# Overlapping the local attention of two batches in a fused two-layer kernel

## The chip, the cores and the metric

The kernel runs on one core of a Trainium2 chip. The metric is the device time of one execution in microseconds; lower is better. Times are told as the median of several runs, and one more execution was taken by the hardware profiler.

## What is computed

The input is x, 8 batches of 512 tokens with 128 channels. Each of two layers is `x = x + s(xn) * silu(f(xn))` with `xn = layernorm(x)`. Only layer 0 has local attention, and the change is mostly there:

```python
# layer 0, s: windowed attention in 64 channels, two branches of 32 channels
xi = rmsnorm(x @ down_w + down_b, norm1_w)
o1 = branch(xi[..., :32], window=10, shift=5)     # 8 heads of 4, relative bias, mask at the wrap
o2 = branch(xi[..., 32:], window=20, shift=10)
x  = x + concat(o1, o2) @ up_w + up_b
s  = x + gelu(rmsnorm(x) @ ffn_w1 + ffn_b1) @ ffn_w2 + ffn_b2
# layer 0, f: 8 experts, the best 2 for each token, and a shared expert (swiglu, width 128)
f  = sum_e cw[t, e] * expert_e(xn[t]) + shared(xn[t])
# layer 1: s is full attention of 16 heads, f is a mixture of 8 experts (width 352), the best 2
```

In a branch, each window of w tokens has a w x w score table for each head: scores plus bias, -100 where the shift has wrapped tokens of both ends into the last window, then softmax, times v, and a projection.

## The kernel before

Tokens lie on partitions, 128 at a time, so a batch is 4 tiles (NT) and all is 32 tiles (TILES). For the windowed attention a batch is folded into 4 groups of windows, so that (group, channel) fill the 128 partitions and the score tables lie along the free dimension in one tile `WS` of 1300 (window 10) + 2800 (window 20) elements.

`plan0()` writes out the order of layer 0 by hand as one list. It begins with statistics, normalisation and the down projection of all batches, then `("route",)`, the routing of all tokens, then a row of slots, which are simply concatenated. Each engine walks the same list and does its own part of each item, in order, with semaphores between engines. So an item that waits holds back everything behind it on that engine.

The items of the slots:

- `("window", b, n)`, n = 0..18 (`FRONT` = 19 slots, one batch after another). n = 0 to 2: the rmsnorm of `XIR` (VectorE squares and sums, GpSimd takes the power, VectorE scales into `XI`). n = 3, 4: TensorE transposes, ScalarE evacuates to `XIT`, TensorE makes q, k, v, ScalarE evacuates to `QKV`. n = 5 to 11: ten chunks; for a chunk, VectorE multiplies q and k into `G` (line 1350), TensorE sums over a head's channels with `HEADSUM` into bank 4 or 5 of PSUM (line 623), VectorE adds the bias into `WS` (line 1341). In a chunk's life these are at slots n, n+1 and n+2. n = 10, 11: VectorE adds `MASK` to the last window on 32 partitions (line 1307) and takes the maximum of each row (1308); GpSimd subtracts it for window 20 (1099), VectorE for window 10. n = 12, 13: ScalarE exponentials. n = 13, 14: VectorE sums and reciprocals (1312, 1314), and for window 10 also the product with v and the output. n = 15: GpSimd multiplies with v for window 20 (1105). n = 18: VectorE's last reduction (1320).
- `("tail", b, k)`, k = 0..6 (`TAIL_AT`): projection, up projection and residual, rmsnorm (ScalarE squares, GpSimd power, VectorE scale), transposes, the two halves of ffn1 with gelu, ffn2. `up_b` and `ffn_b2` are added by a matmul with one row (`ONES` x `ROWS`, lines 572 and 656).
- expert passes k = 0..30: 8 for the shared expert, 23 over blocks of 512 sorted rows. A pass is `sorted` (transposes), `pair` (8 matmuls, line 673), `gate` (two evacuations by ScalarE, two by VectorE at 1393, two clamps at 1397 and 1400, a silu by ScalarE), `act` (1407), `down_e` (TensorE, line 691) and `yev` (VectorE, 1420). Passes begin every 4, 5, 5, 5 slots.
- `("send", g)`: GpSimd issues two indirect DMAs (line 1124), one tile of tokens to its place among the sorted rows. `("split", b)` prepares the weights of layer 1: ScalarE rounds, VectorE subtracts (1425), SyncE stores.

The heart of the plan:

```python
for n in range(FRONT):
    slots[FRONT * b + n].append(("window", b, n))
...
slots[at].append(("pair", k)); slots[at + 1].append(("gate", k)); slots[at + 3].append(("act", k))
slots[at + 5].append(("down_e", k)); slots[at + 6].append(("yev", k))
at += (4, 5, 5, 5)[k % 4]
```

One batch's scores, its `QKV` tile and banks 4 and 5 are single, so the next batch's q, k, v come only after this batch's output. Layer 1 has a plan of the same kind; its routing is one item at slot `ROUTE_AT` = 50, and GpSimd waits there for the positions.

Of the kernel before, what the change touches and what calls it, by code (L numbers as in the profile page):

```python
# [28 lines left out]
FRONT = 19  # L29
# [21 lines left out]
TAIL_AT = {1: 0, 3: 1, 5: 2, 7: 3, 9: 4, 11: 5, 13: 6}  # L51
# [5 lines left out]
def plan0():  # L57
# [9 lines left out]
    out.append(("route",))  # L67
    count = FRONT * B + 40
# [24 lines left out]
def plan1():  # L93
# [23 lines left out]
    put(ROUTE_AT, ("route",))  # L117
    for g in range(TILES):
        put(ROUTE_AT + 2 + g, ("send", g))
# [68 lines left out]
def turns0(plan):  # L188

    uses = []  # L190
    for what, *a in plan:
        if what == "norm":
            uses.append(("xnt", a[0]))
        elif what == "route":
# [3 lines left out]
        elif what == "tail" and a[1] != 2:  # L198
            uses.append((("proj", "up", None, "h", "ffn1a", "ffn1b", "ffn2")[a[1]], a[0]))
# [3 lines left out]
def turns1(plan):  # L203

    uses = []
    for what, *a in plan:
        if what == "norm":
            uses.append(("xnt", a[0]))
        elif what == "route":
# [30 lines left out]
def build(nc, A):  # L240
    ctx = ExitStack()
    with ctx:
# [21 lines left out]
        NHALF = sb("NHALF", [128, NT])  # L264
# [8 lines left out]
        VAR = sb("VAR", [128, NT])  # L273
# [12 lines left out]
        with ExitStack() as one:  # L286
# [12 lines left out]
            UPW = sb0("UPW", [64, 128])  # L299
            ROWS = sb0("ROWS", [1, 3, 128])  # L300
# [3 lines left out]
            MASK = [sb0(f"MASK{r}", [128, WIN[r], WIN[r]]) for r in range(2)]  # L304
# [8 lines left out]
            ZERO = sb0("ZERO", [128, 1024])  # L313
# [5 lines left out]
            TH = sb0("TH", [128, 2, T])  # L319
            YE = sb0("YE", [128, 2, NT, 128])  # L320
            XIR = sb0("XIR", [128, TILES, 64])
            SQT = sb0("SQT", [128, NT, 64])
            SQ = sb0("SQ", [128, 2, NT])
            RSTD = sb0("RSTD", [128, 3, NT])
            XI = sb0("XI", [128, NT, 64])
            XIT = sb0("XIT", [64, XIT_W])
            QKV = [sb0(f"QKV{r}", [128, 3, GRP[r]]) for r in range(2)]
            G = sb0("G", [128, 2, 512])
            WS = sb0("WS", [128, S_W])
            WM = [sb0(f"WM{r}", [128, GRP[r]]) for r in range(2)]  # L330
            WO = [sb0(f"WO{r}", [128, GRP[r]]) for r in range(2)]
            PPT = sb0("PPT", [64, T])
# [74 lines left out]
        def _(sp):  # L407
# [25 lines left out]
            load(ROWS[:], A["rows"], "w_b")  # L433
# [748 lines left out]
        def _(dve):  # L1182
# [140 lines left out]
            def window(b, n):  # L1323
# [27 lines left out]
                if n == 10:  # L1351
                    window_max(1)
# [310 lines left out]
```

## Time and profile before

| | |
|---|---|
| median of 3 runs | 1742.53 us (1740.51 to 1747.9) |
| the profiled execution | 1744.1 us, of which 1742.3 us are the span of the profile |
| VectorE busy | 1111.4 us (64%) |
| TensorE busy | 1167.2 us (67%), mean granted clock 0.765 |
| ScalarE busy | 684.7 us (39%) |
| GpSimd busy | 453.8 us (26%) |
| down projections of all batches end | 63 us |
| routing ends, first window item | 90 us |
| period of one batch in layer 0 | 78.5 us, the same for six batches |
| end of layer 0 | 738.5 us |

A busy share is a mean over stages; in layer 0 the six equal periods between 206 and 678 us are the part to look at. TensorE's busy time depends on its granted clock, 0.5 or 1.0 of 2.4 GHz at any moment; a mean lies between.

### The profile page before, as it was taken

How to read it: one execution, taken by the hardware profiler on the slowest of the kernel's cores; microseconds unless marked ns; L12 is line 12 of the kernel's file. 1: busy time of each engine (PE TensorE's matmuls, PEld its weight loads, DVE VectorE, ACT ScalarE, POOL GpSimd, SP SyncE). 2: the span in 40 equal slices, each digit the busy share in tenths (PEclk: the TensorE clock that was granted, in tenths of full speed). 3: DMA queues.
4: the chain of work that ended last, by engine and by line, in shares of the span. 5: the costliest groups of instructions: out<-in, count | busy, mean ns of one | idle time of the engine just before them, and what ended most of it. 6: DMA issues, size and time to landing. Idle time of an engine off the chain costs nothing.

```text
span 1742.3 us, 17058 instructions
## 1 busy us (share of the span) xinstructions
PE 1167.2 (67%) x5494; PEld 630.5 (36%) x5494; DVE 1111.4 (64%) x1856; ACT 684.7 (39%) x1166; POOL 453.8 (26%) x412
## 2 busy tenths in 40 slices
PE   4464665757585765532456647699997778787886
PEld 4332333434343432311122222288882323232331
DVE  3566758585857657215577586466667878677761
ACT  1112333333323333120223436443445766656663
POOL 2156611120202111243444147500003303213110
PEclk9967868777777868555556769599998888788885
DMA  8210212121221110016033124556544333253400
GB/s 281 101 59 27 71 52 67 43 83 33 83 67 58 62 40 29 6 26 81 17 56 50 18 44 98 113 169 200 200 150 74 49 45 55 41 77 45 73 20 7
DMA packets 73726, 125.03 MB, mean 72 GB/s; under 512 B 13541, under 2 KB 31014, under 8 KB 73638
## 3 DMA queue, kind: packets, MB, share of 16 engines
q1 hardware_dynamic: 65446, 107.15, 25.5%
q0 software_dynamic: 8192, 16.79, 4.0%
q8 instruction: 44, 0.72, 0.2%
q14 instruction: 44, 0.36, 0.1%
HBM read 57.74 MB, written 40.37 MB: 56 GB/s over the span
## 4 chain that ended last, share of the span: by engine, by line
PE 42%; DVE 23%; issue 12%; POOL 10%; ACT 8%; DMA 3%; SPq 2%; DVEq 0%; ACTq 0%; POOLq 0%
PE PS L770 5%; PE PS L813 5%; PE PS L673 5%; PE PS L623 4%; POOL XS1D L1163 4%; PE PS L790 4%; PE PS L832 4%; PE PS L573 3%; ACT P L880 3%; PE PS L750 2%; DVE MX L1553 2%; DVE WS L1307 2%; POOL YG L1147 2%; PE PS L578 2%; PE PS L736 2%
## 5 line engine op out<-in xcount | busy, mean ns | idle before, releaser
L1553 DVE TENSOR_REDUCE MX<-PS 128x1 f32<-128x512 f32 x512 | 323.8, 685 | 132.5 <-PE PS L750 123.5
L880 ACT ACTIVATE P<-PS 128x512 f32<-128x512 f32 x512 | 278.0, 596 | 194.8 <-PE PS L790 192.7
L790 PE MATMUL PS<-QS,KS 50*128 50x512 f32 x512 | 138.2, 536 | 103.6 <-ACT P L880 98.1
L750 PE MATMUL PS<-KS,QS 48*128 48x512 f32 x512 | 149.3, 580 | 66.9 <-DVE MX L1553 40.5
L770 PE MATMUL PS<-P,V 128*32 128x512 f32 x1024 | 180.3, 786 | 0.0
L1147 POOL DMA_INDIRECT A<-Y1D,POS x64 | 73.5, 1148 | 281.2 <-DMA Y1D<-YE 190.8
L750 PEld LDWEIGHTS PS<-KS,QS 48*128 48x128 f32 x512 | 58.0, 224 | 218.7 <-DVE MX L1553 112.6
L790 PEld LDWEIGHTS PS<-QS,KS 50*128 50x128 f32 x512 | 60.0, 230 | 165.5 <-ACT P L880 138.8
L623 PE MATMUL PS<-G,HEADSUM 128*128 128x400 f32 (+2 forms) x160 | 81.2, 639 | 51.5 <-DVE WS L1341 50.6
L673 PE MATMUL PS<-XST,WB 128*128 128x512 f32 x184 | 106.2, 732 | 4.4 <-issue 4.4
L813 PE MATMUL PS<-XRH,WH 128*128 128x512 f32 (+1 forms) x276 | 103.1, 414 | 0.2 <-DVE A L1495 0.2
L1169 POOL TENSOR_TENSOR MAG<-MAG,EH 128x1024 f32<-128x1024 f32 x8 | 19.0, 2369 | 265.2 <-ACT MAG L880 216.7
L1105 POOL TENSOR_TENSOR WS<-WS,QKV 128x2800 f32<-128x2800 f32 x8 | 48.8, 6102 | 131.8 <-DVE WM L1312 131.8
L1099 POOL TENSOR_TENSOR WS<-WS,WM 128x2800 f32<-128x2800 f32 x8 | 39.5, 4940 | 165.1 <-DVE WM L1308 165.1
L1350 DVE TENSOR_TENSOR G<-QKV 128x400 f32<-128x400 f32 (+1 forms) x80 | 46.1, 586 | 54.4 <-PE PS L623 48.9
L1124 POOL DMA_INDIRECT XS0D<-XN,POS x64 | 64.7, 1011 | 54.5 <-issue 52.8
L832 PEld LDWEIGHTS PS<-W,A 128*128 128x128 f32 (+1 forms) x552 | 71.9, 191 | 6.5
L832 PE MATMUL PS<-W,A 128*128 128x128 f32 (+1 forms) x552 | 72.4, 274 | 0.0
L880 ACT ACTIVATE TH<-PS 128x512 f32<-128x512 f32 (+1 forms) x69 | 41.2, 598 | 76.3 <-PE PS L813 76.2
L880 ACT ACTIVATE H<-PS,WB 128x512 f32<-128x512 f32 x46 | 30.9, 687 | 101.5 <-PE PS L673 101.5
L1491 DVE SCALAR_TENSOR_TENSOR SL<-TH,PS 128x512 f32<-128x512 f32 (+1 forms) x69 | 47.1, 683 | 36.1 <-ACT TH L880 36.1
L691 PE MATMUL PS<-WB,AA 128*128 128x128 f32 x184 | 35.5, 354 | 51.7 <-DVE AA L1407 51.7
(208 smaller groups left out, 2222.3 us busy)
## 6 DMA issues: line engine op xcount, KB each, us to landing
WH<-W1SD SPq DMA_DIRECT2D x23, 704.0 KB, 4.3
QS<-EH SPq DMA_DIRECT2D x64, 128.0 KB
KS<-EH SPq DMA_DIRECT2D x64, 128.0 KB
WB<-in_wb SPq DMA_DIRECT2D x23, 322.0 KB, 2.8
XS<-XS0D SPq DMA_DIRECT2D x23, 256.0 KB, 2.7
Y0D<-YE SPq DMA_DIRECT2D x23, 256.0 KB, 2.0
XS<-XS1D SPq DMA_DIRECT2D x23, 256.0 KB, 3.7
Y1D<-YE SPq DMA_DIRECT2D x23, 256.0 KB, 2.7
```

Of the source, the lines that this page charges most:

```text
L623: signal(pe.matmul(PS[:, 4 + c % 2, 0:width], HEADSUM[:], G[:, c % 2, 0:width], start=True, stop=True), "S")
L673: ins = pe.matmul(PS[:, 2 * pair + m, :], w[:, at:at + 128], x, start=True, stop=True)
L750: signal(pe.matmul(PS[:, s % 4, :], QS[rows, u % 3, hp, 128 * t:128 * t + 128], KS[rows, u % 3, hp, :], start=True, stop=True), "ms")
L770: ins = pe.matmul(PS[32 * a:32 * a + 32, 6, :], V[:, u // 2 % 2, k, at:at + 32], P[:, m % 2, a, :], start=k == 0, stop=k == NT - 1)
L790: signal(pe.matmul(PS[:, 4 + s % 2, :], KS[rows, u % 3, hp, 128 * k:128 * k + 128], QS[rows, u % 3, hp, :], start=True, stop=True), "st")
L813: ins = pe.matmul(out, WH[:, j % 2, w, f:f + m], x[:, j % 2, :], start=n == 0, stop=n == 2)
L832: ins = pe.matmul(PS[:, 4 + j % 2, 128 * t:128 * t + 128], A4[0:m, q % 3, 128 * t:128 * t + 128], W2[0:m, j % 2, c, :], start=c == 0 and t ...
L880: act.activation(*a, **k).then_inc(sem[name], 1)
L1124: pool.indirect_dma_start(XS0D, bass.IndirectOffsetOnAxis(POS[0][:, k, g:g + 1], 0), XN[:, g, :], None).then_inc(sem["sent"], 16)
L1147: pool.indirect_dma_start(dst[:, k, t, :], None, src, bass.IndirectOffsetOnAxis(pos[:, k, g:g + 1], 0)).then_inc(sem[name], 16)
L1163: pool.indirect_dma_start(XS1D, bass.IndirectOffsetOnAxis(POS[1][:, k, g:g + 1], 0), XN[:, g, :], None).then_inc(sem["sent1"], 16)
L1553: go("mx", dve.tensor_reduce(MX[:, u % 2, t, 4 * par + hp:4 * par + hp + 1], PS[:, s % 4, :], AX.X, ALU.max))
```

## The change

- The plan of layer 0 has a period: the window items of batch b begin at slot `PERIOD * b` with `PERIOD` = 9 and still take 19 slots, so items of two or three batches share a slot, the older batch first. `WS` and `QKV` have two buffers. The tail of a batch has 8 steps at slots 19 to 27 of it.
- Passes begin every 3 slots, and their items follow each other in neighbouring slots. With `PERIOD` = 9 that is 3 passes in a period.
- The rmsnorm after the down projection is done once for all 32 tiles, in a new item `("xi",)` ahead of the slots, in place in `XIR`. GpSimd then builds the bias tables, too.
- The mask is added to the bias of the last window ahead of time (`LAST`), so that the addition in the chunk's evacuation takes it along; the two additions at line 1307 go.
- The one-row matmuls go: `up_b` is a 65th row of `UPW` against a row of ones in `PPT`; `ffn_b2` is added to `X1` by GpSimd (tail step 3).
- The subtraction of `split` moves from VectorE to GpSimd.
- The routing is in 7 parts in slots 0 to 6 (in layer 1: 50 to 56); the sends begin at slot 8, two tiles in a slot (in layer 1: at 58 rather than 52, one in a slot), and GpSimd waits for the positions only there. The trigonometric tables of layer 1 move from ahead of the slots to slot 27.
- `window_sum` and what follows it come one slot later. `TH` is gone, the silu writes in place.

```diff
-FRONT = 19
+FRONT, PERIOD = 19, 9
-TAIL_AT = {1: 0, 3: 1, 5: 2, 7: 3, 9: 4, 11: 5, 13: 6}
+TAIL_AT = {0: 0, 1: 1, 2: 2, 4: 3, 5: 4, 6: 5, 7: 6, 8: 7}
+ROUTE_PARTS = 7
...
-    out.append(("route",))
+    out.append(("xi",))
...
-            slots[FRONT * b + n].append(("window", b, n))
+            slots[PERIOD * b + n].append(("window", b, n))
         for n, k in TAIL_AT.items():
-            slots[FRONT * (b + 1) + n].append(("tail", b, k))
-        slots[FRONT * b + 9].append(("split", b))
+            slots[PERIOD * b + FRONT + n].append(("tail", b, k))
+        slots[PERIOD * b + 9].append(("split", b))
+    for n in range(ROUTE_PARTS):
+        slots[n].append(("route", n))
     for g in range(TILES):
-        slots[g].append(("send", g))
+        slots[ROUTE_PARTS + 1 + g // 2].append(("send", g))
+    slots[ROUTE_PARTS + 20].append(("trig",))
...
-        slots[at + 3].append(("act", k))
-        slots[at + 5].append(("down_e", k))
-        slots[at + 6].append(("yev", k))
-        at += (4, 5, 5, 5)[k % 4]
+        slots[at + 2].append(("act", k))
+        slots[at + 3].append(("down_e", k))
+        slots[at + 4].append(("yev", k))
+        at += (3,3,3)[k % 3]
```

```diff
 # TensorE, tail: the one-row matmuls
-                    signal(tok_matmul(ntok(out), PPT, UPW[:], ROWS[:, 0]), "aux_full")
+                    signal(tok_matmul(ntok(out), PPT, UPW[:]), "aux_full")
...
-                        pe.matmul(out[:, t], ONES[0:1, :], ROWS[:, 1], start=True, stop=False)
 # VectorE, window: the mask
-                step(dve.tensor_tensor(s, s, MASK[r][96:128].rearrange("p q k -> p (q k)"), ALU.add))
...
+                        if w <= (PADT // WIN[r] - 1) % NWIN[r] < w + m:
+                            bias = LAST[r][:].rearrange("p w q k -> p w (q k)")
+                        else:
+                            bias = bc(BIAS[r][:].rearrange("p q k -> p (q k)"), [128, m, a], 1)
 # ScalarE, window n = 4: q, k, v of the next batch no longer wait for this one's output
-                    if b:
-                        act.wait_ge(sem["wout0"], b)
-                        act.wait_ge(sem["wout1"], b)
+                    if b >= 2:
+                        act.wait_ge(sem["wout0"], b - 1)
+                        act.wait_ge(sem["wout1"], b - 1)
 # GpSimd
+                elif what == "xi":
+                    pool.wait_ge(sem["xi_sq"], 1)
+                    rsqrt(RSTDX[:], SQX[:], 1.0 / 64, 1e-6, "rstd_xi")
...
+                        go("init_p", pool.tensor_tensor(last, last, bc(BIAS[r][:].rearrange("p q k -> p (q k)"),
+                                                                       [128, (3, 1)[r], w * w], 1), ALU.add))
...
+                elif what == "tail" and a[1] == 3:
+                    pool.wait_ge(sem["h0"], a[0] + 1)
+                    go("x1_b", pool.tensor_tensor(X1[:], X1[:], bc(FB2[:], [128, NT, 128], 1), ALU.add))
+                elif what == "split":
+                    pool.wait_ge(sem["split_hi"], a[0] + 1)
+                    go("split_lo", pool.tensor_tensor(SPL[:], STAGE[:], SPH[:].bitcast(F32), ALU.subtract))
 # VectorE, once for all tiles
+                    step(dve.tensor_tensor(sq, XIR[:], XIR[:], ALU.mult))
+                    go("xi_sq", dve.tensor_reduce(SQX[:], sq, AX.X, ALU.add))
+                    dve.wait_ge(sem["rstd_xi"], 1)
+                    go("xi", dve.tensor_tensor(XIR[:], XIR[:], bc(RSTDX[:], [128, TILES, 64], 2), ALU.mult))
+                    dve.wait_ge(sem["init_p"], 5)
```

## Rows read from the trace of the kernel before

**Rows 1.** Windows: busy us of each engine, instructions, granted TensorE clock, DMA share, GB/s.

```profile
285.07:363.60 78.53, 52.30 (x222) 30.67 (x221) 53.07 (x65) 25.93 (x43) 13.46 (x7) 0.76 0.20 62
...
718.30:747.00 28.70, 12.80 (x32) 7.42 (x32) 2.08 (x3) 4.62 (x12) 7.68 (x9) 0.50 0.05 13
...
1003.00:1022.50 19.50, 5.27 (x20) 2.17 (x20) 14.52 (x48) 3.61 (x8) 0.01 (x1) 0.59 0.00 0
```

**Rows 2.** Groups of VectorE from 90 to 745 us: busy us, mean ns, idle before.

```profile
L1393 DVE SCALAR_TENSOR_TENSOR UL<-PS,WB,H 128x512 f32<-128x512 f32 x46 | 33.4, 747 | 30.2 <-ACT H L880 30.2
L1307 DVE TENSOR_TENSOR WS<-WS,MASK 32x100 f32<-32x100 f32 x8 | 32.5, 4066 | 0.3
...
L1407 DVE SCALAR_TENSOR_TENSOR AA<-UL,TH 128x512 f32<-128x512 f32 x31 | 21.3, 686 | 2.5 <-DVE X L1372 2.1 <-ACT TH L880 0.4
...
L1400 DVE TENSOR_SCALAR UL<-UL 128x512 f32<-128x512 f32 x31 | 13.0, 418 | 0.0
...
L1314 DVE RECIPROCAL WM<-WM 128x140 f32<-128x140 f32 x8 | 8.2, 1028 | 0.3
...
L1425 DVE TENSOR_TENSOR SPL<-STAGE,SPH 128x704 fp32r<-128x704 f32 x8 | 7.1, 884 | 0.0
...
L1307 DVE TENSOR_TENSOR WS<-WS,MASK 32x400 f32<-32x400 f32 x8 | 4.6, 571 | 0.3
```

**Rows 3.** Timeline, VectorE and GpSimd in one period: start us, length us.

```profile
285.07 4.08 DVE L1307 TENSOR_TENSOR WS<-WS,MASK 32x100 f32<-32x100 f32 x1
...
312.63 1.23 DVE L1397 TENSOR_SCALAR UL<-UL 128x512 f32<-128x512 f32 x1
...
284.10 4.94 POOL L1099 TENSOR_TENSOR WS<-WS,WM 128x2800 f32<-128x2800 f32 x1 [25.06 <-DVE WM L1308]
307.47 6.11 POOL L1105 TENSOR_TENSOR WS<-WS,QKV 128x2800 f32<-128x2800 f32 x1 [18.43 <-DVE WM L1312]
```

**Rows 4.** Timeline of TensorE in one period.

```profile
644.40 2.92 PE L610 MATMUL PS<-XIT,WQKV 64*32 64x130 f32 x48 [0.93 <-ACT XIT L880]
...
649.10 5.90 PE L673 MATMUL PS<-XST,WB 128*128 128x512 f32 x8 [0.73 <-issue]
...
663.60 3.01 PE L623 MATMUL PS<-G,HEADSUM 128*128 128x400 f32 x4 [1.84 <-DVE WS L1341]
...
674.55 3.60 PE L673 MATMUL PS<-XST,WB 128*128 128x512 f32 x8
...
696.94 2.08 PE L691 MATMUL PS<-WB,AA 128*128 128x128 f32 x8 [12.86 <-DVE AA L1407]
```

**Rows 5.** Groups of ScalarE from 90 to 745 us.

```profile
L880 ACT ACT_TABLE_LOAD x30 | 38.5, 1283 | 0.5
...
L880 ACT ACTIVATE WS<-WS 128x1300 f32<-128x1300 f32 x8 | 10.3, 1286 | 0.1
```

**Rows 6.** Groups of GpSimd from 90 to 745 us.

```profile
L1124 POOL DMA_INDIRECT XS0D<-XN,POS x64 | 64.7, 1011 | 54.5 <-issue 52.8 <-POOL RSTD L1078 0.6 <-POOL WS L1099 0.6
...
L1078 POOL TENSOR_TENSOR RSTD<-VAR,NHALF 128x4 f32<-128x4 f32 x8 | 8.2, 1020 | 0.7
```

**Rows 7.** A group of TensorE from 90 to 745 us (that of line 572 is alike).

```profile
L656 PE MATMUL PS<-ROWS,ONES 1*128 1x128 f32 x64 | 16.7, 343 | 6.2 <-ACT GL L880 6.2
```

**Rows 8.** Timeline: bias copies, last down projection, first and last step of routing, layer's end.

```profile
49.33 4.28 POOL L1117 COPY BIAS<-RPB 128x10 f32<-128x10 f32 x30
...
62.91 0.42 DVE L1459 TENSOR_TENSOR XIR<-PS,DOWNB 128x256 f32<-128x256 f32 x1 [2.99 <-PE PS L573]
...
68.46 0.42 DVE L1224 TENSOR_REDUCE RS<-PS 128x32 f32<-128x256 f32 x1
...
89.57 0.42 DVE L1284 TENSOR_REDUCE GW<-RT 128x32 f32<-128x256 f32 x1
...
737.85 0.69 DVE L1382 TENSOR_TENSOR XN<-PS,X 128x512 f32<-128x512 f32 x1 [15.32 <-PE PS L658]
```

**Rows 9.** Timeline of VectorE in layer 1, after the sends.

```profile
1116.62 1.23 DVE L1543 CAST EH<-MAG 128x2048 fp32r<-128x2048 f32 x1 [10.01 <-POOL MAG L1170]
```

More of the change, by code:

```diff
@@ L197, in turns0 @@
             uses.append(("xs", a[0]))
-        elif what == "tail" and a[1] != 2:
-            uses.append((("proj", "up", None, "h", "ffn1a", "ffn1b", "ffn2")[a[1]], a[0]))
+        elif what == "tail" and a[1] not in (2, 3):
+            uses.append((("proj", "up", None, None, "h", "ffn1a", "ffn1b", "ffn2")[a[1]], a[0]))
     return {use: n for n, use in enumerate(uses)}
@@ L303, in build @@
             BIAS = [sb0(f"BIAS{r}", [128, WIN[r], WIN[r]]) for r in range(2)]
-            MASK = [sb0(f"MASK{r}", [128, WIN[r], WIN[r]]) for r in range(2)]
+            LAST = [sb0(f"LAST{r}", [128, (3, 1)[r], WIN[r], WIN[r]]) for r in range(2)]
             FW1 = sb0("FW1", [128, 256])
@@ L567, in aux, with tok_matmul @@
                 return PS[:, 7, :]
-            def tok_matmul(out, lhs, rhs, row=None):
+            def tok_matmul(out, lhs, rhs):
                 for t in range(NT):
-                    if row is not None:
-                        pe.matmul(out[:, t], ONES[0:1, :], row, start=True, stop=False)
-                    ins = pe.matmul(out[:, t], lhs[:, 128 * t:128 * t + 128], rhs, start=row is None, stop=True)
+                    ins = pe.matmul(out[:, t], lhs[:, 128 * t:128 * t + 128], rhs, start=True, stop=True)
                 return ins
@@ new lines, in route @@
+                if part == 4:
+                    ps, free = bank_filled(dve, "prefix") if L else (aux_filled(dve, "prefix"), sem["aux_free"])
+                    freed = (SHARED if L else AUX)["prefix",] + 1
+                    counts = lambda n: ps[:, TILES * E * n:TILES * E * (n + 1)].rearrange("p (t e) -> p t e", e=E)
+                    dve.wait_ge(sem["hot" + pre], 1)
+                    dve.tensor_copy(RT[:, 6], counts(0))
+                    step(dve.tensor_copy(RT[:, 7], counts(1)))
+                    dve.tensor_copy(RT[:, 5], counts(1)).then_inc(free, 1)
+                    dve.wait_ge(free, freed)
+                    at, to = 7, 8
+                    for s in (1, 2, 4, 8, 16):
+                        dve.tensor_copy(RT[:, to, 0:s], RT[:, at, 0:s])
+                        step(dve.tensor_tensor(RT[:, to, s:], RT[:, at, s:], RT[:, at, 0:TILES - s], ALU.add))
+                        at, to = to, at
@@ new lines, in route @@
+                if part == 6:
+                    for k in range(2):
+                        step(dve.tensor_tensor(RT[:, 8], RT[:, 3 + k], RT[:, 7], ALU.mult))
+                        step(dve.tensor_reduce(RS[:, k], RT[:, 8], AX.X, ALU.add))
+                        go("pos" + pre, dve.tensor_copy(POS[L][:, k], RS[:, k]))
+                        dve.wait_ge(sem["pos" + pre], k + 1)
+                    for k in range(2):
+                        step(dve.scalar_tensor_tensor(RT[:, 8], RT[:, 3 + k], scale, RT[:, 1], ALU.mult, ALU.mult))
+                        go("gw" + pre, dve.tensor_reduce(GW[L][:, k], RT[:, 8], AX.X, ALU.add))
+                        dve.wait_ge(sem["gw" + pre], k + 1)
@@ L1344, in window @@
                         r, w, m = CHUNKS[c]
-                        q, kk = (QKV[r][:, j, :].rearrange("p (w q) -> p w q", q=WIN[r])[:, w:w + m] for j in range(2))
+                        q, kk = (QKV[r][:, b % 2, j, :].rearrange("p (w q) -> p w q", q=WIN[r])[:, w:w + m] for j in range(2))
                         full = [128, m, WIN[r], WIN[r]]
@@ L1476, in _ @@
                     expert_out(*a)
-                elif what == "split":
-                    split(*a)
             layer0_over(dve)
```

315 lines of the change are left out of this document (147 added, 168 removed).

## The prediction

> **What bounds the kernel now.** I read the windows by stage first, then the groups of each engine in layer 0, then the timeline of one period engine by engine, and last the chain that ended last. Layer 0's slots run from 90 to 738.5 us [rows 8]. Six batches there take 78.5 us each, the same to a hundredth; one of them is [rows 1], first row. In it VectorE is busy for 53.1 of 78.5 us and TensorE for 52.3, at a granted clock of 0.76. So no engine is full. The reader should see in the same row that ScalarE (25.9) and GpSimd (13.5) are far from full too: what bounds the period is the alternation of in-order queues, with 25.4 us in which VectorE waits. After the last window there is a stretch that nothing covers: from 718 to 738 us VectorE is busy for 2.1 us and TensorE runs at 0.50 (second row) [rows 1]. And from 63 to 90 us VectorE does tables and routing alone [rows 8].
>
> **A lock that is easily missed.** The mask addition on 32x100 elements takes 4.07 us, that on 32x400 elements 0.57 us [rows 2]. The small one starts at 285.07 us while GpSimd's subtraction (284.10 to 289.04) is running, and ends with it, at 289.15 [rows 3]. A clamp beside GpSimd's product takes 1.23 us in place of 0.42 and ends when that ends [rows 2, 3]. So a GpSimd tile operation holds back VectorE operations that read two SBUF tiles, and clamps, until it is over. The evacuations (PSUM and SBUF) ran beside it unharmed. The Trainium skill says the same in "SBUF — State Buffer", section "SBUF: two separate sides": the pair of ports that VectorE and GpSimd share is an exclusive lock held for a whole instruction. The trace agrees (4.07 against 0.57 us). By that rule the two operations that this change gives to GpSimd are not free for VectorE wherever a product stands beside them; the sum below counts the lock from the rows.
>
> **The change, VectorE's work.** From 53.07 us in a period go: the mask additions, 4.07 + 0.57 [rows 2]; the split's subtraction, 0.88 [rows 2]; the rmsnorm of XI, three operations on 128x256 at 0.42, 1.26 [rows 8]; the blocked part of a clamp, 1.23 - 0.42 = 0.81 [rows 3]; and one pass in four, since a period now has 3 passes: 2 x 0.747 + 2 x 0.418 + 2 x 0.686 (yev is as long as act) = 3.70 [rows 2]. That leaves 41.8 us.
>
> **Its waits.** I walk through the 9 slots of a period (numbered 1 to 9) in the order of the queues (older batch, younger batch, pass), starting at the end of the gate in the third slot.
> (a) Slots 4 to 6: VectorE has act, h0 and the sum, product and output of window 10, but these need the exponential. ScalarE has the silu, four squares, a table load of 1.28 and the exponential of 1.29 first [rows 5]. Wait at least 1.3; with the squares I take 3.0. The chain XIT, 2.92 us of q, k, v matmuls [rows 4], QKV ends at about the same time as this VectorE work, so it is hidden.
> (b) The gate in slot 6 waits for its pair, which stands behind those 48 matmuls and a down_e on TensorE. TensorE has idled before, so I take the pair of 5.90, not of 3.60 [rows 4], and down_e at 2.08: wait 4.3.
> (c) Slot 7: the sum over window 20 releases GpSimd's product of 6.1 us [rows 3]. Behind the sum VectorE has the reciprocal (1.03 [rows 2]) and then the q, k products of the younger batch, which read two SBUF tiles. They stand for 6.1 - 1.0 = 5.1 us.
> (d) Slot 9: products 6 and 7 need the sums of chunks 4 and 5, which stand on TensorE behind chunks 2 and 3 (up to 3.0 for two [rows 4], here 2.1), down_e 1.7, a pair of some 5.5, half of ffn1 and their own matmul, some 1.6: 12 us after the lock opens. VectorE has 5.3 us of its own meanwhile: wait 6.6.
> (e) Slot 3: the up projection stands behind down_e and a pair (4.7, between the two of [rows 4]), 8.4 us in all against 4.4 us of VectorE's: wait 4.0.
> Period: 41.8 + 3.0 + 4.3 + 5.1 + 6.6 + 4.0 = 64.8, taken as 65. What TensorE is spared is mostly in its shadow: the one-row matmuls are 16.7 + 16.7 us in all [rows 7], 4.2 a batch, of which only the four in front of the up projection are in (e). GpSimd's new operations: at 4.94 us for 2800 elements [rows 3], 704 take 1.2 and 512 take 0.9. They fall beside evacuations and reductions as I lay it out, so I cost them at nothing; if that cover is gone they cost their length. For GpSimd itself, 13.5 us a period grows by 2 in 65.
>
> **Start.** XIR is complete at 63.3 [rows 8]. Two small operations 0.4, squares and sum over 2048 elements, each between the 1.23 of a cast of that size [rows 9] and 8 x 0.42 [rows 8], taken as 2.2; GpSimd's power: 1.02 us for 4 columns [rows 6], for 32 columns between that and 8 x 1.02; I take 2, near the floor. Then GpSimd copies the bias, 4.28 [rows 8], which used to be hidden, and adds two LAST tables (700 elements, 1.3 by the rate above). VectorE scales XIR in that time. All queues wait for this: 63.3 + 0.4 + 4.4 + 2.5 + 4.3 + 2.0 = 77, taken as 78 (bounds 76 and 84). So slots start at 78, not at 90, but the routing, 68.5 to 90.0 [rows 8], is now inside them.
>
> **Slots.** There are 96 of them, the last pass being number 30 at 3 x 30 + 1, with its yev four later. Period 0 (routing 19 us, three passes 11, half a window 7, waits 5): 42. Period 1 (no tails): 57. Periods 2 to 7: 65 each, plus 4 in the third, and 3 in the fourth for the tables. The 4 are for the sends: 64 at 1.01 us and 0.3 us between [rows 6], 81 us, plus 22 us of window work in the same queue, 103 us for slots 8 to 23 of the plan (numbered from 0), against about 107 us that the others need there; the first sorted pass stands in slot 24 right behind and still has its rows to load. Period 8 has no young batch: 44. Period 9 has the last tail and three passes: 37. Two more passes: 20. The last store: 3. Sum: 42 + 57 + 6 x 65 + 7 + 44 + 37 + 20 + 3 = 600, so layer 0 ends at 678 rather than 738.5: 60.5 us less. Each us of the period is worth about 7 us.
>
> **Layer 1.** The routing was a block of 19.5 us in which TensorE was busy for 5.3 (third row) [rows 1]; and behind the sends VectorE waited 10.0 us for a GpSimd product that stood behind all of them [rows 9]. In parts, the one is filled by attention, and the product gets in before the last sends. Against it, positions come later and the sends begin 6 slots later, and at 81 us their length sets when the first rows can be loaded. Bounds 0 and 20 less; I take 7, near the floor, since the sends bind.
>
> **Sum.** 1744.1 - 60.5 - 7 = 1676.6 for an execution like the profiled one; the median of the runs is 1.6 lower: 1675 us.
>
> **Rivals.**
> 1. TensorE stays fast. It has fewer gaps, its clock rises from 0.76 to near 1, and pairs take 3.6 us: 2.3, 1.9 and 1.1 less in (b), (d), (e), and 0.7 from the chunk sums, 6 in all. Period 59, time 1633. For it: pairs of 3.60 exist. Against: its work falls from 52.3 to about 41 us in 65, so its share (63%) is no higher than now (67%). 24%.
> 2. The waits (a), (b), (d), (e) fall under other work, and VectorE is the bound but for the lock: 41.8 + 5.1 + 2 = 49. Time 1675 - 16 x 7 = 1563. Against: its queue is in order, and each wait above is of one queue on another that can't be overtaken. 7%.
> 3. The lock bites everywhere: GpSimd's subtraction (4.9), split (1.2) and bias (0.9) each meet a product or a clamp. 7 more, period 72, time 1725. For it: in the period now both big GpSimd operations do meet one [rows 3]. 14%.
> 4. The other side: TensorE becomes the bound at half clock. Three pairs at 6, five times 3.0 for the chunks, three down_e at 2.1, 2.9 for q, k, v and some 16 for tail and transposes are 58 us; with the stretches in which it must wait for VectorE's reductions (some 18) the period is 76 and the time 1752. It decides from a period of 75. For it: 0.50 in the lone tail [rows 1]. Against: at the same share of work the clock is 0.76 now. 5%.
> 5. The change doesn't overlap: a bank or a tile that is still single (banks 4 and 5, the shared bank 7, WM, WO) makes the batches follow each other, and the saved operations are paid back by the bunched passes. Time 1742. 3%.
>
> **How the numbers follow.** The forecast as laid out, 1655 to 1700, has 47%, and 1675 is its middle. The range of 8 in 10 reaches over most of rival 1 and a part of rival 3: 1620 to 1715. It takes in the bounds of start and layer 1 (+6, +7 and -13) and 5 us of the period either way. A measurement of this kernel can tell about 0.5%, 9 us, from no change. Faster by more: 47 + 24 + 7 + 14 = 92%; within: 3%; slower: 5%.
>
> **What would show it.** Slots start (first routing step) near 78 us. Six periods of about 65 us. VectorE near 42 us plus blocked time in each. The younger batch's third product takes some 5 us or starts late, beside GpSimd's product. Products 6 and 7 wait for TensorE by 6 to 7 us. Granted clock near 0.76. Layer 0 ends near 678. In layer 1 no wait of 10 us behind the sends. The prediction is wrong if the period is not 60 to 70, most likely by (b), (d) and (e), which hang on pairs between 3.6 and 5.9 us.

## The result, and the profile after

The changed kernel takes 1710.75 us (median of 4 runs, 1708.24 to 1715.08), the kernel before, on the same chip, 1741.52 us (median of 4 runs, 1736.76 to 1747.9). The ratio is 0.983, 95% interval 0.980 to 0.986: 31 us less, where the prediction had 67. The time lies inside the range of 1620 to 1715, near its upper end.

The windows of the changed kernel, in the columns of [rows 1]: the first slots; from the row maximum of window 20 of one batch to that of the next (batches 0 to 7, to within 0.3 us); the last batch; the end of layer 0; layer 1.

```profile
82.64:126.00 43.36, 26.04 (x108) 14.59 (x108) 33.56 (x85) 10.42 (x20) 4.13 (x4) 0.80 0.02 7
131.18:188.81 57.63, 32.80 (x142) 18.78 (x140) 48.34 (x51) 15.66 (x23) 47.51 (x37) 0.68 0.14 48
188.81:265.50 76.69, 39.30 (x181) 23.70 (x180) 49.11 (x66) 23.07 (x41) 41.91 (x31) 0.70 0.26 83
265.50:334.30 68.80, 41.38 (x185) 24.90 (x184) 47.13 (x54) 22.72 (x39) 15.19 (x6) 0.69 0.18 56
334.20:399.50 65.30, 36.68 (x173) 22.23 (x173) 47.16 (x54) 22.86 (x39) 15.16 (x6) 0.74 0.18 58
399.50:467.50 68.00, 39.39 (x199) 24.42 (x196) 47.17 (x54) 23.30 (x40) 15.16 (x6) 0.75 0.18 58
467.50:532.70 65.20, 36.58 (x174) 22.18 (x174) 47.19 (x54) 22.87 (x39) 15.17 (x6) 0.74 0.18 59
532.70:600.90 68.20, 39.23 (x187) 24.05 (x185) 47.13 (x54) 23.08 (x39) 15.16 (x6) 0.73 0.16 51
600.90:668.00 67.10, 42.55 (x158) 25.47 (x154) 39.03 (x38) 22.18 (x33) 13.50 (x5) 0.72 0.14 44
668.00:708.70 40.70, 25.76 (x88) 15.44 (x88) 14.76 (x26) 13.79 (x26) 2.50 (x4) 0.81 0.14 49
708.70:1706.40 997.70, 723.14 (x3622) 356.46 (x3622) 645.44 (x1171) 475.93 (x821) 263.90 (x241) 0.76 0.35 75
```

Read down the first figure after the window. The 78.53 us of a batch [rows 1] have become 65 to 69 in the last five of these periods, so the overlap is real. The two ahead of them, in which GpSimd issues the sends, take 57.6 and 76.4 (to the row maximum itself). In the last five VectorE's busy time is 47.1 us, the same each time; what varies is what it waits for. The last four alternate, 65 and 68 us. Layer 0 ends at 708.7 us, not 738.7 (738.5 above was VectorE's last operation, this is GpSimd's first of layer 1) and not 678; layer 1 takes 997.7 us, before 1742.3 - 738.7 = 1003.6. So of the 36 us by which the forecast was too low, 30.7 lie in layer 0 and 1.1 in layer 1 (forecast 996.6); the rest is that this execution lies below the median of the runs and the one of before above its own.

The timeline of the start, VectorE and GpSimd (before: [rows 8]):

```profile
74.17 2.29 DVE L1481 TENSOR_TENSOR XIR<-XIR,RSTDX 128x2048 f32<-128x2048 f32 x1 [5.93 <-POOL RSTDX L1084]
82.64 0.42 DVE L1244 TENSOR_REDUCE RS<-PS 128x32 f32<-128x256 f32 x1 [6.18 <-POOL LAST L1127]
...
68.72 5.43 POOL L1084 TENSOR_TENSOR RSTDX<-VAR,NHALF 128x32 f32<-128x32 f32 x1
74.21 3.49 POOL L1124 COPY BIAS<-RPB 128x10 f32<-128x10 f32 x10
...
81.59 1.03 POOL L1127 TENSOR_TENSOR LAST<-LAST,BIAS 128x400 f32<-128x400 f32 x1
```

VectorE stands twice, 5.93 us for GpSimd's power on 32 columns (5.43 us) and 6.18 us for the tables behind it. The first ten bias copies take 3.49 us beside VectorE's scaling of `XIR` (74.17 to 76.46). One of them takes 2.31 us, where the median is 0.20: here VectorE's operation holds GpSimd's.

The timeline of VectorE in one period, 533 to 601 us, some of the rows that waited or were held (in brackets the idle time ahead and its releaser), with GpSimd's product:

```profile
541.84 0.69 DVE L1388 TENSOR_TENSOR X<-PS,XN 128x512 f32<-128x512 f32 x1 [6.23 <-PE PS L575]
...
569.79 6.07 DVE L1366 TENSOR_TENSOR G<-QKV 128x400 f32<-128x400 f32 x2
...
586.43 1.28 DVE L1366 TENSOR_TENSOR G<-QKV 128x400 f32<-128x400 f32 x2 [4.63 <-PE PS L625]
...
568.87 6.08 POOL L1110 TENSOR_TENSOR WS<-WS,QKV 128x2800 f32<-128x2800 f32 x1 [13.89 <-DVE WM L1331]
```

The two products of q and k, 1.05 us without a neighbour, take 6.07 together and end 0.9 us after GpSimd's product (568.87 to 574.95): that is the lock, about 5.0 us. The waits of VectorE in the two periods from 467.5 to 600.9 us, grouped (us in total, times, longest):

```profile
DVE G L1366 <- PE PS L625: 17.7, 10, 4.6
DVE X L1388 <- PE PS L575: 9.8, 2, 6.2
DVE H L1393 <- POOL SCALES L1084: 3.9, 2, 1.9
DVE UL L1410 <- PE PS L674: 2.1, 2, 1.1
DVE UL L1410 <- ACT H L883: 1.9, 2, 1.0
```

Nearly half of all waiting (19.6 us a period) is for chunk sums (L625), in 5 places of each period, not only in the one of step (d).

The period with most of the sends, 188.8 to 265.2 us, has waits of its own (timeline of VectorE, then of TensorE):

```profile
202.10 3.25 DVE L1414 TENSOR_SCALAR UL<-UL 128x512 f32<-128x512 f32 x1
...
211.75 0.69 DVE L1393 TENSOR_TENSOR H<-X,SCALES 128x512 f32<-128x512 f32 x1 [5.02 <-POOL SCALES L1084]
...
239.71 1.18 DVE L1366 TENSOR_TENSOR G<-QKV 128x400 f32<-128x400 f32 x2 [9.73 <-PE PS L625]
...
234.49 1.09 PE L580 MATMUL PS<-IDENT,XS 128*128 128x128 f32 x4 [12.01 <-DMA XS<-XS0D]
```

TensorE stands 12.0 us for the rows of the first sorted pass, whose load is issued at 231.7 us, just behind the last send (230.4), and the chunk sum that VectorE wants stands behind it in the same queue (9.7 us). GpSimd's power comes late behind sends (5.0 us, later 1.9), and so does its subtraction, which then meets a clamp (3.25 us, else 0.42).

### The profile page after: what moved, and what is told of

It is laid out like the page before. It is cut to its first block, busy times and chain, and to the rows that moved or that the text cites. A ratio compares the mean times of both kernels' runs of the same rounds, so it can differ in the third digit from the quotient of the medians.

```text
span 1706.4 us, 16795 instructions
## 1 busy us (share of the span) xinstructions
PE 1121.3 (66%) x5366; PEld 607.4 (36%) x5366; DVE 1099.5 (64%) x1815; ACT 682.4 (40%) x1166; POOL 479.8 (28%) x417
## 4 chain that ended last, share of the span: by engine, by line
PE 40%; DVE 18%; POOL 13%; issue 10%; ACT 9%; DMA 3%; SPq 1%; DVEq 0%; ACTq 0%; POOLq 0%
PE PS L816 6%; PE PS L674 5%; PE PS L773 5%; PE PS L793 4%; POOL XS1D L1180 4%; PE PS L835 4%; POOL XS0D L1135 4%; PE PS L625 3%; ACT P L883 3%; POOL YG L1164 2%; PE PS L753 2%; DVE MX L1572 2%; PE PS L692 2%; PE PS L739 2%; DVE UL L1410 2%
## 5 line engine op out<-in xcount | busy, mean ns | idle before, releaser
L625 PE MATMUL PS<-G,HEADSUM 128*128 128x400 f32 (+2 forms) x160 | 93.0, 720 | 108.8 <-DVE WS L1357 108.8
L1366 DVE TENSOR_TENSOR G<-QKV 128x400 f32<-128x400 f32 (+1 forms) x80 | 75.6, 962 | 72.1 <-PE PS L625 71.5
L674 PE MATMUL PS<-XST,WB 128*128 128x512 f32 x184 | 94.2, 659 | 1.5 <-issue 1.5
L625 PEld LDWEIGHTS PS<-G,HEADSUM 128*128 128x128 f32 x160 | 38.2, 258 | 145.7 <-issue 140.9
L1135 POOL DMA_INDIRECT XS0D<-XN,POS x64 | 67.2, 1050 | 47.5 <-issue 45.5
L1180 POOL DMA_INDIRECT XS1D<-XN,POS x64 | 64.1, 1002 | 49.5 <-DVE POS L1302 30.3
L1509 DVE SCALAR_TENSOR_TENSOR SL<-TH,PS 128x512 f32<-128x512 f32 (+1 forms) x69 | 47.1, 683 | 36.9 <-ACT TH L883 36.9
L612 PE MATMUL PS<-XIT,WQKV 64*32 64x130 f32 (+1 forms) x384 | 22.6, 417 | 72.8 <-ACT XIT L883 72.8
```

The lines of the kernel that those rows point to most:

```text
L625: signal(pe.matmul(PS[:, 4 + c % 2, 0:width], HEADSUM[:], G[:, c % 2, 0:width], start=True, stop=True), "S")
L674: ins = pe.matmul(PS[:, 2 * pair + m, :], w[:, at:at + 128], x, start=True, stop=True)
L1135: pool.indirect_dma_start(XS0D, bass.IndirectOffsetOnAxis(POS[0][:, k, g:g + 1], 0), XN[:, g, :], None).then_inc(sem["sent"], 16)
L1180: pool.indirect_dma_start(XS1D, bass.IndirectOffsetOnAxis(POS[1][:, k, g:g + 1], 0), XN[:, g, :], None).then_inc(sem["sent1"], 16)
```

## The experiments

Twelve experiments ran, in three groups (one is the changed kernel itself, one a repetition). In each group the kernel before ran on the same chip (7 runs), and ratios are to it. Its median was 1740.79 us in the first group, 1835.49 in the second and 1841.53 in the third. The second and third ran on other chips, on which layer 1 of the changed kernel takes about 70 us longer (1067.0 us in the third group) and the kernel before about 100 in all, but layer 0 is no longer: where it is unedited it ends at 708.7 us in the execution above and at 709.4, 710.3 and 710.2 in the other groups. So I compare layer 0 by its end in the trace, and whole times only within a group.

### Group 1: where does the gain come from, and what do lock and start cost?

**One batch after another.** All edits stay but the overlap; the passes go back to their old distances with it.

```diff
-FRONT, PERIOD = 19, 9
+FRONT, PERIOD = 19, 19
...
-        slots[at + 2].append(("act", k))
-        slots[at + 3].append(("down_e", k))
-        slots[at + 4].append(("yev", k))
-        at += (3,3,3)[k % 3]
+        slots[at + 3].append(("act", k))
+        slots[at + 5].append(("down_e", k))
+        slots[at + 6].append(("yev", k))
+        at += (4, 5, 5, 5)[k % 4]
```

> Everything of the change but the overlap: batches follow each other every 19 slots and passes are spaced 4, 5, 5, 5 with the old distances. Theory A (the period is work plus the waits of in-order queues, so each removed operation counts for what it took): before's period of 78.5 loses 4.6 for the masks, 0.9 for the split, 2.8 for the rmsnorm chain and 1.5 to 3 for the rows, about 68; with the start at 83 and the routing inside, 1670, which is faster than the whole change: then the overlap costs more than it gives, since 31 passes at 3 in 67 us take longer than 8 batches at 68. Rival (the overlap carries the gain and the small edits hide in waits): period 76 or more, 1725 or more.

Measured: 1755.06 us, ratio 1.009 (1.007 to 1.010); layer 0 ends at 758.0 (in a profiled execution 12 us above the median). Theory A falls, and the rival holds: without the overlap, the saved operations bring no gain. One batch takes 79.1 us, before 78.5:

```profile
465.40:544.50 79.10, 48.63 (x206) 28.87 (x204) 50.98 (x59) 28.71 (x45) 15.51 (x6) 0.74 0.19 61
```

VectorE is busy for 51.0 us, not for 53.07 less the 4.64 of the masks, 0.88 of the split, 1.26 of the rmsnorm and 0.81 of the blocked clamp, which is 45.5. The timeline of its VectorE shows where 5.4 of that went:

```profile
393.61 3.79 DVE L1373 TENSOR_TENSOR WS<-WS,WM 128x1300 f32<-128x1300 f32 x1
...
414.87 3.52 DVE L1414 TENSOR_SCALAR UL<-UL 128x512 f32<-128x512 f32 x1
```

The mask addition had stood behind the lock (4.07 us, [rows 2]). With it gone, the next operation that reads two SBUF tiles, window 10's subtraction, comes there and takes 3.79 instead of 1.51; the clamp takes 3.52 instead of 0.42. 2.3 + 3.1 = 5.4 us: the lock was not removed, it found other work. And the less VectorE does, the earlier it stands before TensorE (6.19 us for the up projection in this version). The loss of 14 us against the kernel before lies elsewhere, in the second batch, which takes 103.1 us (126.55 to 229.64) where the kernel before takes 77.0 (125.34 to 202.35). The sends are two in a slot here, and the power of the first tail stands behind them:

```profile
194.66 0.69 DVE L1393 TENSOR_TENSOR H<-X,SCALES 128x512 f32<-128x512 f32 x1 [14.88 <-POOL SCALES L1084]
```

So the overlap, with its passes at even distance, is worth 1755.1 - 1710.8 = 44 us with the sends as they are now. How much of the 44 is that the overlap bears the bunched sends better was not run; in the equal periods alone it is 79.1 against 66.7 us.

**GpSimd's product left out.** The kernel multiplies 20 elements instead of 2800, so its output for window 20 lacks the product with v.

```diff
+                    s = s[:, 0:1, 0:1, :]
-                    go("wpv1", pool.tensor_tensor(s, s, bc(v, [128, NWIN[1], w, w], 2), ALU.mult))
+                    go("wpv1", pool.tensor_tensor(s, s, bc(v[:, 0:1], [128, 1, 1, w], 2), ALU.mult))
```

> GpSimd's product with v for window 20 is left out but for 20 elements (the output is then not the reference's). Theory A: the lock of 5.0 us on VectorE's products is on the path in every period: period 61.7 in place of 66.7, total 1671. Rival 1 (TensorE's chain takes over at once): half of it, 1690. Rival 2 (the lock is in a shadow): within 5 us of 1711.

Measured: 1676.48 us, ratio 0.962 (0.960 to 0.965); layer 0 ends at 669.7, 39 us earlier, some 5 us a batch. Theory A has the numbers: its period was 61.7, and the last three are 61.5. But not all of it is the lock. These periods are all of the short kind (group 3 tells what that is), and against the short periods of the changed kernel, 65.2, they are 3.7 us less; the rest is that the long ones are gone. The waits for chunk sums remain, 19.4 us in two periods, so they don't come from the lock.

**VectorE makes this product.** The line moves behind the sum over window 20, in VectorE's queue.

```diff
 # VectorE, behind window_sum(b, 1); gone from GpSimd
+                    go("wpv1", dve.tensor_tensor(s, s, bc(v, [128, NWIN[1], WIN[1], WIN[1]], 2), ALU.mult))
```

> The same product is done by VectorE behind its sum instead of by GpSimd. VectorE works 3.0 us more in a period and is not locked out for 5.0: theory A says 2 us less a period, total 1695. Rival (VectorE's time is dear everywhere, the lock is partly hidden): 3 us more a period, 1735.

Measured: 1694.04 us, ratio 0.973 (0.971 to 0.975), as expected; layer 0 ends at 694.6, 14.1 us earlier. VectorE needs 3.1 us for what GpSimd needs 6.1 for, and GpSimd's 6.1 held VectorE for 5.0. The offloaded operation cost the engine that it was to relieve more than doing it. The gain is not spread evenly, though: the last three equal periods are 64.9 us each, 0.3 less than the short ones of the changed kernel and 3.3 less than its long ones, and 5.6 of the 14.1 us lie behind the last row maximum, where GpSimd's product had held an act of VectorE (5.70 us instead of 0.69).

**Bias tables ahead of the power.** GpSimd copies the bias and adds `LAST` before it waits for the sums of squares.

```diff
 # GpSimd, item ("xi",)
-                    pool.wait_ge(sem["xi_sq"], 1)
-                    rsqrt(RSTDX[:], SQX[:], 1.0 / 64, 1e-6, "rstd_xi")
                     pool.wait_ge(sem["w_b"], 16 * 18)
...
+                    pool.wait_ge(sem["xi_sq"], 1)
+                    rsqrt(RSTDX[:], SQX[:], 1.0 / 64, 1e-6, "rstd_xi")
```

> GpSimd builds the bias tables ahead of its wait for the sums of squares. Theory A: slots start when XIR is scaled, 76.5 us in place of 82.6, and all behind it comes 6 us earlier: 1705. Rival (the first passes or the sends set the pace there): no change.

Measured: 1700.57 us, ratio 0.978 (0.976 to 0.979). Slots start at 77.7 instead of 82.6 and layer 0 ends 6.3 earlier, so the start is in full on the path. No bias copy takes over 0.21 us here. The medians are 10.2 us apart; the 4 us more lie behind layer 0, and nothing here explains them.

### Group 2: which wait is the period's, and what are the small edits worth?

**Passes one slot later.**

```diff
-    at = 1
+    at = 2
     for k in range(PASSES):
```

> Passes begin at slot 2 of the plan rather than at slot 1, nothing else. The pair then stands behind the up projection and behind the sums of chunks 4 and 5 in its slot, and ahead of others. Theory A (a wait is where a pair stands ahead of something VectorE needs): waits (e) 3.6 to 6.2 and (d) 4.6 go, a wait for chunks 6 and 7 and one for the projection come: 3 us less a period, 1690. Rival (waits only move): within 8 us of 1711.

Measured: 1766.73 us, ratio 0.9615 (0.958 to 0.9645); layer 0 ends at 696.2, 12.5 us earlier. The waits of VectorE in two of its periods, 455.8 to 585.5 us:

```profile
DVE G L1366 <- PE PS L625: 15.9, 14, 2.7
DVE XN L1399 <- PE PS L659: 8.9, 2, 4.7
...
DVE X L1388 <- PE PS L575: 2.4, 1, 2.4
```

The up projection is no longer behind a pair (9.8 us become 2.4), but now ffn2 is (0 become 8.9). The period goes from 66.7 to 64.9 only, 1.8 us where theory A had 3, and the rival (within 8 us) falls, too. I read it so that TensorE has three pairs a period to put somewhere and some wait follows each; that is argued, not tried. Another 6.9 of the 12.5 us come in one period, that behind the sends (264.0 to 326.0 us, 62.0 long instead of 68.9).

**Mask additions back,** as additions of a zero table on the same 32 partitions, in the old place.

```diff
+                s = WS[96:128, b % 2, S_AT[r] + lastw * w * w:S_AT[r] + (lastw + 1) * w * w]
+                step(dve.tensor_tensor(s, s, ZERO[96:128, 0:w * w], ALU.add))
```

> The two additions on 32 partitions are made again at their old places (they add zeros). Theory A: in the new order they fall behind the wait for the up projection, when GpSimd's subtraction is over, so they cost their work, 0.7 us a period: 1717. Rival (the lock comes back with them, as before the change, 4 us more): 1745.

Measured: 1786.96 us, ratio 0.974 (0.969 to 0.978); layer 0 ends at 714.0, 5.3 us later. In the new layout the two take 0.57 and 0.26 us, and nothing is held: the 4.07 us were a matter of place, not of the addition. Theory A's 6 us are met by luck. In the long periods the addition ahead of the row maximum disappears in the wait for the up projection (5.65 us instead of 6.23), and the period stays 68.2 to 68.3; 3.1 of the 5.3 us are that one period, short in the changed kernel, is long here.

**One-row matmuls back,** with a zero row, four ahead of up and four ahead of ffn2 in a batch.

```diff
 # ahead of each of the four matmuls of up, and of the four pairs of ffn2
+                        pe.matmul(out[:, t], ONES[0:1, :], ZERO[0:1, 0:128], start=True, stop=False)
```

> The one-row matmuls are made again ahead of the up projection and ffn2 (with a row of zeros). Theory A: only the four ahead of the up projection are waited for, 1.5 us a period: 1722. Rival 1: all of them count, 4.2 us a batch: 1745. Rival 2: none: 1711.

Measured: 1821.23 us, ratio 0.990 (0.986 to 0.994); layer 0 ends at 749.2, 40.5 us later. Theory A (12) falls; rival 1 (34) is nearest. These eight small matmuls are the largest of the small edits. The period is 71.7 us throughout. The timeline of TensorE ahead of the up projection in this kernel:

```profile
563.51 3.60 PE L677 MATMUL PS<-XST,WB 128*128 128x512 f32 x8
567.04 0.48 PE L576 MATMUL PS<-ZERO,ONES 1*128 1x128 f32 x2
567.45 0.49 PE L577 MATMUL PS<-UPW,PPT 65*128 65x128 f32 x2
...
569.95 0.49 PE L577 MATMUL PS<-UPW,PPT 65*128 65x128 f32 x2
```

and in the changed kernel:

```profile
537.31 3.60 PE L674 MATMUL PS<-XST,WB 128*128 128x512 f32 x8
540.75 1.06 PE L575 MATMUL PS<-UPW,PPT 65*128 65x128 f32 x8
```

With the rows between, the projection takes 3.4 us instead of 1.06, and VectorE's wait for it is 8.3 us every time.

**Routing of layer 1 in one slot,** sends at slot 52 again.

```diff
-        put(ROUTE_AT + n, ("route", n))
+        put(ROUTE_AT, ("route", n))
...
-        put(ROUTE_AT + ROUTE_PARTS + 1 + g, ("send", g))
+        put(ROUTE_AT + 2 + g, ("send", g))
```

> In layer 1 alone, the parts of the routing stand in one slot again and the sends begin at slot 52. GpSimd still waits for the positions only at the first send. Theory A: the 6 us that layer 1 gained come from the parts in equal shares with the GpSimd product that no longer stands behind the positions: 3 to 6 us more, 1716. Rival: the later sends cost as much as the parts gain, no change.

Measured: 1793.42 us, ratio 0.976 (0.9735 to 0.979). The changed kernel itself did not run on this chip, and layer 1 differs between chips by more than the effect: this run decides nothing on layer 1. It was run again in group 3.

### Group 3: the changed kernel beside its variants

**The changed kernel again,** without an edit.

> The changed kernel itself, beside the kernel before and the three others of this group on one chip, so that they can be compared with it and not only with the kernel before. Expected: ratio to the kernel before 0.983 if the chip is like the first, 0.975 if it is like the one of the second group (layer 1 longer by 75 us, layer 0 the same); layer 0 ends at 708.7 us in either case.

Measured: 1782.85 us, ratio 0.973 (0.963 to 0.983), as expected for such a chip; layer 0 ends at 710.3, expected 708.7.

**Three edits together:** bias tables early, the product on VectorE, passes one slot later (the three diffs above).

> Three edits that each made layer 0 shorter, together: bias tables built ahead of the wait for the sums of squares (alone 6.3 us), VectorE makes the product of window 20 with v itself (alone 14.1 us), passes one slot later (alone 12.5 us). Theory A, the gains are of different waits (start, lock, up projection) and add up: layer 0 ends at 708.7 - 33 = 676, ratio to the changed kernel 0.981. Rival, product and phase lie in the same place, since passes one slot later already move the work of the younger batch away from the product of GpSimd or put its pair behind the chunk sums: only 20 us or less, layer 0 ends at 688 or later.

Measured: 1744.56 us, ratio 0.9505 (0.941 to 0.960), and 1744.56 / 1782.85 = 0.979 of the changed kernel. Layer 0 ends at 675.4, where theory A had 676, and 34.9 us ahead of the changed kernel on the same chip. The gains add up. One of its periods (61.5 us), and the waits of VectorE in two, from 441.85 to 564.73 us:

```profile
503.20:564.70 61.50, 41.63 (x185) 25.24 (x184) 44.93 (x54) 25.66 (x41) 9.78 (x5) 0.72 0.17 57
```

```profile
DVE XN L1396 <- PE PS L659: 10.9, 2, 5.4
DVE G L1360 <- PE PS L625: 10.3, 10, 1.3
DVE X L1385 <- PE PS L575: 4.8, 2, 2.4
```

The long waits of step (d) are gone (the longest is 1.3 us), and the price is ffn2 behind a pair, 5.4 us. This version is faster than both kernels.

**Only the rows ahead of up.**

> Only the four one-row matmuls ahead of the up projection are back, with a zero row, not those of ffn2. Both together had moved the end of layer 0 by 40.5 us, while they themselves are 2 x 1.3 to 2.1 us a batch. Theory A, as the prediction has it: only those ahead of the up projection are on the path, so this alone gives most of the 40.5: layer 0 ends at 735 or later. Theory B, each costs by its own and half of the loss is from ffn2's: about 728. Theory C, the loss came from TensorE's clock, which the rows of both together push to the low level in every period: below 722 here, with the alternation of 65 and 68 us still there.

Measured: 1796.85 us, ratio 0.981 (0.971 to 0.990); layer 0 ends at 720.4, 10 us later. Theory A falls, and B too. C has the right size (below 722), but the alternation that was to be its sign is gone, every period is 68.3 us. That is no point against C, as the clock below shows:

```profile
543.60:611.90 68.30, 40.19 (x193) 24.48 (x193) 47.15 (x54) 23.06 (x40) 15.16 (x6) 0.75 0.16 50
```

The wait for the up projection tells what happened. In the changed kernel it is 3.6 and 6.2 us in turn: in the long periods the projection and the chunk sum ahead of it take 1.90 and 2.96 us, in the short ones 1.05 and 1.61. The four rows add 2.4 (3.4 against 1.06). With the up rows alone it is 6.0 in every period, which is 3.6 + 2.4, and the chunk sum takes 1.61: all periods are of the short kind, plus rows. With the rows of ffn2 too it is 8.3 in every period, nearly 6.2 + 2.4, and the two take 1.90 and 2.58: all periods are of the long kind. With the 0.95 us that VectorE now waits for ffn2 itself, this is 3.2 of the 3.4 us between the periods of 68.3 and 71.7. So the rows ahead of up cost 10 us, less than 2.4 a period since the long periods turned short, and those of ffn2 the other 30, most of it by what they do to the matmuls after them.

What makes TensorE quick or slow at that place is its granted clock. These are the windows over projection and chunk sum, the clock third from the end: a short and a long period of the changed kernel, then the version with up rows, then that with both.

```profile
466.10:468.80 2.70, 2.66 (x26) 2.06 (x27) 2.63 (x4) 0.68 (x1) 0.00 (x0) 1.00 0.37 101
531.70:536.60 4.90, 4.87 (x26) 3.51 (x27) 3.84 (x3) 0.68 (x1) 0.85 (x1) 0.52 0.16 54
...
542.40:544.90 2.50, 2.50 (x25) 1.90 (x26) 2.43 (x3) 0.68 (x1) 0.00 (x0) 1.00 0.29 107
...
558.30:562.60 4.30, 4.29 (x24) 3.12 (x25) 3.81 (x3) 0.68 (x1) 0.28 (x1) 0.55 0.23 65
```

The short course has the high level (2.4 GHz) there, the long one the low level (1.2 GHz). In both TensorE had stood for 6.3 us and then begun a chunk sum at the low level; in the short period the clock is at 1.00 from the transposes on (464.8 us), ahead of the projection, in the long one only behind the chunk sum (536.4 us). The transposes, the projection and the chunk sum are 0.5, 0.9 and 1.4 us longer, 2.7 in all, and VectorE waits 2.6 us longer for the up projection. So theory C has the mechanism: with both kinds of rows the clock is low there in all three periods looked at, with the up rows alone it is high in all three. What lets the clock rise earlier in one period than in the next was not tried and stays open.

**Routing of layer 1 in one slot, again.**

> Routing of layer 1 in one slot with the sends at slot 52, as before the change, now with the changed kernel on the same chip. Theory A of the prediction: routing in parts is worth 7 us (bounds 0 and 20), so this is 7 us slower than the changed kernel and layer 1 longer by as much. Rival: the sends start six slots earlier here and bind what follows, so it is no slower, 0 to 5 us faster.

Measured: 1794.57 us, ratio 0.9775 (0.967 to 0.988), beside 1782.85 of the changed kernel: 12 us more by the medians, 13.4 in layer 1 of the profiled executions (1080.4 against 1067.0). The intervals overlap, so size and sign are not shown by the times; the traces have the sign of the prediction, and nothing speaks for the rival.

## Why the prediction was right or wrong

The direction was right, and so was the mechanism of the overlap (queues in order, waits that shrink); the gain was less than half of the forecast, and no rival describes what came. The steps, one by one.

**VectorE's work, right.** 47.1 us busy a period, of which 5.0 are the lock: 42.1 against 41.8.

**The waits, right in sum, wrong in parts.** Forecast 3.0 + 4.3 + 5.1 + 6.6 + 4.0 = 23.0. Measured: (a) 0.8 and 1.9 behind ScalarE and GpSimd, 2.7; (b) 1.1 + 1.0 = 2.1, since the pair takes 4.0 us there and not 5.9; (c) 5.0; (d) 4.6; (e) 3.6 and 6.2 in turn, mean 4.9, and 0.3 for what hangs on it; and one that was not in the list, the other chunk sums, 1.3 + 0.7 + 1.3 + 0.9 = 4.2, where the forecast let VectorE pass freely. Together 23.8, and the period is 66.7 (mean of the last four) against 65. That the two sums agree within 1 us is luck: 2.2 and 2.0 less in (b) and (d) stand against 4.2 more for the other chunk sums and 1.2 in (e).

**Where it failed:** in four terms of the sum of the slots, "taken as 78", "Period 1 (no tails): 57" with the "plus 4 in the third" for the sends, "65 each", and "Period 8 has no young batch: 44".
- The start, 82.6 against 78, 4.6 us. GpSimd's power on 32 columns took 5.43 us, and I had taken 2, "near the floor"; the row of 1.02 us for 4 columns allowed 8.2. And "VectorE scales XIR in that time" left out that the lock works the other way, too: the copies took 6.3 us and not 4.3, since one of them was held for 2.1. Of these 5.5 us about 1 was covered, since the sum of 77 had been rounded up to 78. The experiment with early bias tables shows that these microseconds pass through.
- The two periods with the sends, 57.6 + 76.4 = 134.0 against 57 + 65 + 4 + 3 = 129 (the tables, 4.6 us of VectorE, end just ahead of the next row maximum), 5.0 us. The first is right. In the second the rows of the first sorted pass come 12 us late for TensorE, and power and subtraction stand behind sends. Another execution divides them otherwise, 64.9 + 70.2, with nearly the same sum.
- The five equal periods behind them, 335.6 against 5 x 65 = 325, 10.6 us. The short ones take 65.2 and are as forecast. The long ones take 68.0 to 68.9, three times: the low clock at the projection and the chunk sum makes (e) 5.9 to 6.3 us where the sum had 4.0.
- Period 8, 55.9 us from one up projection (610.09) to the next (666.03) against 44. VectorE is busy for 34.4 of it: the younger batch's work is gone, but not the waits. An act stands in the lock (5.70 instead of 0.69 us), down_e and a pair of 4.85 us follow it, and VectorE waits 6.2 us for ScalarE behind that pair and 9.0 for the up projection. In the last 40.7 us of the layer it is busy for 14.8, and the waits are pair, ScalarE's evacuation and down_e in turn, with 3.2, 5.4 and 4.6 us at single places; that end and period 0 are otherwise near the forecast. Period 0 and all behind 600.8 us take 156.4 against 42 + 44 + 37 + 20 + 3 = 146, 10.4 us.

4.6 + 5.0 + 10.6 + 10.4 = 30.6 us, but for rounding the whole error in layer 0 (30.7). Most of it is size, and each was taken at its friendly side; two mechanisms the sum did not have, GpSimd held by VectorE at the start and the clock that differs from one equal period to the next.

**The clock (rival 1), wrong as a rival and half right as a doubt.** The mean granted clock is 0.69 to 0.75 in the equal periods, as forecast and not near 1. But in the last four the pairs take 3.6 to 4.2 us, nearly as rival 1 had it; the slow stretches fall on chunk sums and projections instead, and which of them are slow makes the 3 us between the periods.

**The lock (rival 3).** In the equal periods only the product holds VectorE. The subtraction falls into the wait for the up projection, split (1.67 us) and the addition of `FB2` (1.26) beside row sums, and nothing is held by them. In the two periods with the sends the subtraction comes late and holds a clamp, 4.26 and 3.25 us instead of 0.42, so rival 3 is true there. The Trainium skill has the rule, in "SBUF — State Buffer", section "SBUF: two separate sides", that the shared ports are locked for a whole instruction; the trace agrees with 6.07 us for 1.05 us of work. Not in the prediction was that with each edit other work stands behind the lock: in the version without overlap 5.4 us came back that way.

**The other side (4) and no overlap (5).** TensorE is busy for 36.6 to 41.4 us of an equal period, far from 75. The overlap works, 44 us by experiment.

**What TensorE is spared, mis-sized.** "Mostly in its shadow" was wrong: the one-row matmuls are worth 40 us in the new plan, about a third more than the whole gain. The prediction did not need that size, since it counted the kernel without them, but the step that "only the four in front of the up projection are in (e)" was wrong: they give 10 us, those of ffn2 30, mostly by the low clock at the matmuls behind them.

**Layer 1, right on this chip.** 5.9 us less against 7. On the chip of the third group the medians leave some 30 us for it (58.7 in all, 28.4 of them in layer 0, if the kernel before ends layer 0 there at 738.7, too); no trace of the kernel before was taken there, so why is open.

## What to carry to other kernels

Where queues are in order, count an operation by what stands behind it, not by its length: one-row matmuls of 33 us [rows 7] that were thought hidden were worth 40, and the saved operations without the overlap brought nothing (79.1 us a batch, before 78.5). Before an operation is given to GpSimd, ask how long it holds VectorE; here its 6.1 us held VectorE for 5.0, and VectorE would have needed 3.1. And when a plan is costed by an equal period, the parts that are not equal (start, the periods with the sends, end) want the same care: there lay 20 of 31 us of the error.

## What the runs showed of the hardware that was not expected

- GpSimd's power grows with the columns: 1.02 us for 4, 5.43 us for 32 (5.44 in the version with early tables).
- A program of equal periods can alternate between two courses, here 65.2 and 68.2 us in turn, by the granted clock of a few matmuls, 1.00 or 0.52, with the pair behind them at 3.60 us in both. The timeline of TensorE in the short and in the long one:

```profile
466.14 1.05 PE L637 MATMUL PS<-WO,PROJ 128*32 128x130 f32 x16 [0.69 <-ACT XST L883]
...
467.16 1.61 PE L625 MATMUL PS<-G,HEADSUM 128*128 128x500 f32 x4
```

```profile
531.73 1.90 PE L637 MATMUL PS<-WO,PROJ 128*32 128x130 f32 x16 [0.69 <-ACT XST L883]
...
533.62 2.96 PE L625 MATMUL PS<-G,HEADSUM 128*128 128x500 f32 x4
```

- The lock works both ways: a bias copy of GpSimd took 2.31 us instead of 0.20 beside VectorE's product on 128x2048, 2.29 us.
- Between chips, layer 1 of the changed kernel differed by about 70 us and layer 0 by under 2. Why was not looked into.
